# The sums over values ahead of the projections and outputs in TensorE's odd steps

## The reference

```
xn = layernorm(x)
q, k, v = xn @ Wq.T, xn @ Wk.T, xn @ Wv.T          (split into 16 heads)
diff_sq  = max(|q|^2 + |k|^2 - 2 q.k, 0)
cosh_arg = 1 + 2 diff_sq / max((1 - |q|^2)(1 - |k|^2), 1e-6)
attn = softmax(-arccosh(max(cosh_arg, 1)))          (over the 1024 keys)
out  = x + (attn @ v) @ Wo.T + xn @ int4(kernel) + bias + (xn @ a) @ b
```

## Time and profile before

| | |
|---|---|
| median of 3 runs | 2432.23 us (2431.07 to 2434.84) |
| profiled execution | 2431.75 us, of it span 2430.1 us |
| mean granted TensorE clock | 0.993 |
| TensorE (PE) busy | 2259.8 us, 93% |
| ScalarE (ACT) busy | 2166.6 us, 89% |
| VectorE (DVE) busy | 2014.8 us, 83% |
| sum_v matmuls (L223) | 4096, 548.0 us busy |
| sum_one matmuls (L239) | 2048, 270.7 us busy |

### The profile page before, as it was taken

One profiled execution on the slowest core, in us unless ns is written; L12 is line 12 of the kernel. 1 busy time (PEld: TensorE's weight loads), 2 busy tenths in 40 slices (PEclk: granted clock), 3 DMA queues, 4 the chain that ended last, 5 costly groups with the idle time before them and its releaser, 6 DMA issues. The chain is left out here.

```text
span 2430.1 us, 45001 instructions
## 1 busy us (share of the span) xinstructions
PE 2259.8 (93%) x17416; PEld 817.8 (34%) x17416; DVE 2014.8 (83%) x2754; ACT 2166.6 (89%) x2051; POOL 84.5 (3%) x75
## 2 busy tenths in 40 slices
PE   6999999999999999999999999999999999987776
PEld 2433333333333333333333333333333333322222
DVE  7779888888888888888888888888888888876675
ACT  4379999999999998999999999999999999999993
POOL 0100000000000000000000000000000000000000
PEclk9999999999999999999999999999999999999998
DMA  4443334433445443354525344443334454253422
GB/s 154 125 135 84 109 95 130 127 101 108 117 139 130 132 116 91 113 143 126 144 80 137 103 131 135 134 126 105 113 108 144 125 135 109 84 135 91 116 82 80
DMA packets 355425, 285.01 MB, mean 117 GB/s; under 512 B 81132, under 2 KB 294252, under 8 KB 355208
## 3 DMA queue, kind: packets, MB, share of 16 engines
q1 hardware_dynamic: 355208, 282.10, 41.8%
HBM read 159.77 MB, written 121.36 MB: 116 GB/s over the span
## 5 line engine op out<-in xcount | busy, mean ns | idle before, releaser
L508 ACT ACTIVATE root<-pU 128x1024 f32<-128x1024 f32 x1024 | 1030.1, 1027 | 55.3 <-PE pU L211 47.1
L512 ACT ACTIVATE root<-root 128x2048 f32<-128x2048 f32 x512 | 983.1, 1920 | 47.4 <-DVE root L828 46.7
L828 DVE TENSOR_SCALAR root<-root 128x2048 f32<-128x2048 f32 x512 | 625.3, 1221 | 101.5 <-ACT root L508 101.0
L211 PE MATMUL pU<-QS,KS 100*128 100x512 f16 x2048 | 615.7, 383 | 68.9 <-ACT root L508 62.8
L833 DVE TENSOR_TENSOR root<-root 128x2048 f32<-128x2048 f32 x256 | 585.5, 2287 | 43.4 <-PE pO L223 27.1
L223 PE MATMUL pO<-root,VX 128*32 128x512 f32 x4096 | 548.0, 605 | 49.7 <-ACT o_s L518 49.7
L211 PEld LDWEIGHTS pU<-QS,KS 100*128 100x128 f16 x2048 | 145.2, 97 | 602.8 <-ACT root L508 290.6
L239 PE MATMUL pZ<-root,ones 128*32 128x512 f32 x2048 | 270.7, 595 | 0.9 <-DVE root L833 0.9
L291 PE MATMUL pM<-Wqh,xT 128*128 128x512 f16 x480 | 162.8, 383 | 3.1 <-DVE xT L678 1.6
L223 PEld LDWEIGHTS pO<-root,VX 128*32 128x32 f32 x4096 | 84.5, 108 | 233.9 <-issue 223.6
L291 PE MATMUL pM<-Wvh,xT 128*128 128x512 f16 x480 | 161.7, 379 | 0.4 <-DVE Wvl L632 0.4
(11 more groups left out here) (223 smaller groups left out, 2163.2 us busy)
## 6 DMA issues: line engine op xcount, KB each, us to landing
v_d<-v_o SPq DMA_DIRECT2D x64, 264.0 KB, 2.1
k_d<-kx SPq DMA_DIRECT2D x64, 264.0 KB, 2.2
KT<-k_d SPq DMA_DIRECT2D x64, 264.0 KB
VX<-v_d SPq DMA_DIRECT2D x64, 264.0 KB
xts<-in_x SPq DMA_DIRECT2D x32, 512.0 KB, 4.1
res_d<-f_o SPq DMA_DIRECT2D x64, 256.0 KB, 4.0
QS<-qh_d SPq DMA_DIRECT2D x128, 128.0 KB
KS<-kh_d SPq DMA_DIRECT2D x128, 128.0 KB
```

What stands on the lines that cost most here:

```text
L211: mm = pe.matmul(pU[:, col:col + HALF], KS[i][:, h, j * P:(j + 1) * P], QS[i][:, h, half * HALF:(half + 1) * HALF], start=True, stop=True)
L508: act.activation(root[:, q % RING, cols], pU[:, cols], ACT.Square).then_inc(squared, 1)
L512: act.activation(root[:, q % RING, :], root[:, q % RING, :], ACT.Sqrt).then_inc(rooted, 1)
L828: v.tensor_scalar(root[:, q % RING, :], root[:, q % RING, :], CS * CS, CS * CS, ALU.max, ALU.subtract).then_inc(clamped, 1)
```

## The change

In TensorE's program, `behind(p, k)` and the `sum_v` of odd steps change places. Even steps have no `sum_v`, and `sum_one` stays last. No instruction is added, removed or altered, and no other engine's program changes.

```diff
                     distances(0)
                 if s + 1 < 2 * QUADS:
                     distances(s + 1)
-                behind(p, k)
                 if s % 2 and 0 <= (s - 5) // 2 < QUADS:
                     sum_v((s - 5) // 2)
+                behind(p, k)
                 if s % 4 == 1 and 0 <= (s - 7) // 2 < QUADS:
                     sum_one((s - 7) // 2)
```

## The result

The changed kernel takes 2569.67 us (median of 4 runs, 2567.31 to 2570.03), the kernel before 2431.66 us on the same chip: a ratio of 1.0563, 95% interval 1.0544 to 1.0581. 2565 us were forecast, from 2505 to 2592.

The account below looks back on a forecast made before the run. No engine is full; a chain passing between TensorE, ScalarE and VectorE was taken as the bound. 2431.75 us + 98.0 (periods 8 to 55) + 10.5 (periods 1 to 7) + 24.6 (clock) = 2564.9, forecast 2565 us, range 2505 to 2592.

Parts of the forecast that it names:

- The chain enters TensorE at the copies: At ScalarE's pO copies; in period 22 a halved clock made TensorE 1.63 us later, the next copy 1.64 us later.
- Step 5: Six v projection matmuls land behind the wait for the pO copy, delaying step 6's distances: 1.52 us a period.
- Turns: Steps 9 and 13: switching between sums and fp16 matmuls costs two more turns, 0.22 us for each period.
- the late k projection: Step 3, odd periods: k projection ends behind the sums, so ScalarE takes k 0.6 us late, in even-to-odd stretches alone.
- Sum of the stretches: Copy to next copy, 24 even and 24 odd periods: 2.34 and 1.74 us each, 98.0 us together.
- Periods 1 to 7: Periods without outputs: between 0 and 2.34 us each, taken as 1.5, 10.5 us together.
- The clock: Even periods' longer wait drops TensorE's clock in 15 of 23 cases at 1.64 us each: 24.6 us.
- Rival (a): Slower by the other terms, but a 3 us wait does not lower the clock: 2540 us, chance 0.22.
- From period 56 on: Last periods, without projections: nothing stands in step 5, so no loss, 0 us.
- (b): Delay mostly taken back by slack in ScalarE and VectorE: 2468 us, with odd periods' share 2505; chance 0.15.
- (c): Faster: sums end 1.3 us earlier, so VectorE's add_pair waits for them go: 2404.7 us, chance 0.04.
- (d): No difference, because TensorE would idle in step 5 either way: 2432 us, chance 0.04.

Follow-up runs that it names:

- e2: Kernel before with the new order in step 5 alone: 2555.30 us, ratio 1.0511.
- e7: Kernel before with the new order in steps 9 and 13 alone: 2448.66 us, ratio 1.0059.
- e6: Kernel before with the new order in step 3 alone: 2442.28 us, ratio 1.0034.
- e1: Changed kernel with the old order in step 5 alone, the new order in all other odd steps: 2468.41 us, ratio 1.0148 to the kernel before.
- e5: Changed kernel with six extra matmuls, result unread, ahead of step 5's sums in periods 1 to 55: 2548.20 us, ratio 1.0465 to the kernel before.
- e8: Changed kernel with sum_one moved ahead of the product too: 2543.94 us, ratio 1.0449 to the kernel before.
- e9: Changed kernel with the old order from period 56 on: 2560.36 us, ratio 1.0533 to the kernel before.
- e10: Kernel before with the new order from period 56 on alone: 2441.50 us, ratio 1.0041.
- e4: Kernel before with ScalarE's copy of pO one step earlier, in step 4: 2393.91 us, ratio 0.9842.

## Why the prediction was right, point by point

- *The chain enters TensorE at the copies, and a delay behind them is passed on in full.* Right. The accident of period 22 had been the only evidence; the changed kernel repeats it eleven times at 1.6 us each, and e2's three plain stretches are longer by the whole 1.54 us.
- *Step 5: 1.52 us, in even and odd periods.* Right: 3.61 us from the sums to the distances against 3.60. e2's odd-to-even stretches are 34.6 us longer in sum, 1.44 each.
- *Turns, 0.22 us a period, and the late k projection, 0.60.* Right in kind, a little small. e7 measures the turns at 0.33 and 0.24 us, e6 the projection at 0.35 us alone; in e1 the sum is 0.94 instead of 0.82. The 0.26 that e6 and e7 leave fits the turn of step 1, which makes the k projection later still, but no run has that turn alone. ScalarE's wait for k is 0.48 us in the changed kernel.
- *Sum of the stretches.* 2.34 and 1.74 us were forecast; the undisturbed even stretch grew by 2.48 us, the odd ones by 39.7 / 24 = 1.65 in the mean (an undisturbed one by 1.78).
- *Periods 1 to 7.* 13.1 us against 10.5. The price was a guess within 0 and 2.34 us, and its reason, that the copy is waited for in these periods as well, holds in the kernel before for only two of the seven (0.58 us in period 2, 0.20 in period 4).
- *The clock.* Right in kind, too dear in size. Falls in 11 even periods instead of the 15 assumed, each at the price read from period 22. Net of the one fall that the kernel before had, 16.3 us, where 24.6 were in the sum. The mean granted clock of 0.981 misses the sign named in advance, 0.97 or less. Rival (a) held that waits of 3 us do not lower the clock; e5 shows that they do. The wait was 2.72 to 2.99 us, mostly under the 2.9 to 3.1 forecast. The two of three was a guess, and the share of falls isn't set by the length of the wait alone: with 3.08 us and more it was 21 of 23 in e2 and 11 of 23 in e8. e9, with the same code as the changed kernel up to period 55, had 11 falls too, but some in other periods, two of them (10 and 14) behind waits of 2.72 us. What decides beside the length stays open.
- *From period 56 on: 0.* Wrong, and by e9 and e10 worth 9 us. The step of the argument was that nothing stands in step 5 there, and that ScalarE has the chain; it left out that the turns of steps 9 and 13 lengthen TensorE's waits (1.68 instead of 1.49 us), and, as far as argued, that an engine off the chain comes onto it when its clock is halved. This error and the clock's cancelled; without that luck the sum would have been 2574 or 2557.
- *Rivals (b), (c), (d).* Nothing was taken back. ScalarE's wait for the norm fell from 42.8 to 34.4 us only. VectorE's wait for the sums did vanish, from 27.1 to 2.8 us, as (c) had it, and was worth nothing: VectorE waits for squares 174.6 us now, 101.0 before.

## What to carry to other kernels

Work that stands ahead of a wait in an in-order engine's list is free as long as the wait lasts; before moving it, look for which instruction the wait stands at, and count everything that ends up behind it, for the chain takes it at full price. Here the better change was the opposite one, to look at who is being waited for: the copy, one step earlier in ScalarE's list, made the kernel 1.6% faster (e4). And count the turns between kinds of matmul, and whether an idle time gets so long that the clock falls: the turns cost a quarter of a microsecond and come every period, a fall cost 1.6 us and came in 11 of them.

## What the runs showed of the hardware

- Adding 330 useless matmuls, 1.3 us in each of 55 waits, made the kernel 21 us faster (e5 against the changed kernel), since TensorE's granted clock (0.981 to 0.990 in the mean) no longer fell to 1.2 GHz behind the wait.
- In these profiles single waits of the sums up to 1.80 us were not followed by a fall in the projecting periods. Waits of 2.05 and 2.06 us were in some cases (periods 22 of the kernel before and 55 of the changed one) and not in another (period 22 of e6), 2.72 to 2.99 us in 11 of 23, and 3.08 us and more in 21 of 23 (e2) or 11 of 23 (e8). The Trainium skill ("TensorE: Matmul & The Clock Gate", section "Why this matters for your kernels") advises against idle gaps between bursts of matmuls, of a length that among these only e2's and e8's waits reach. The trace agrees in kind, but here shorter waits were followed by falls too.
- A fall costs by how much of the work lies in it: 1.6 us when it begins 0.4 to 1.2 us behind the start of the sums, and in e2, where the sums mostly start at half speed, 1.4 us when the clock is back 3 us behind their start and 2.6 when it takes over 5 us.
- The turn from eight fp32 matmuls in column groups of 32 to fp16 matmuls over all columns and back costs 0.24 to 0.33 us for the pair (e7). The Trainium skill ("TensorEngine Tiling (Array Packing)", section "Key Properties") says that changing the tiling mode drains TensorE; the trace agrees, with 1.00 instead of 0.86 us on the one side and 0.31 instead of 0.22 on the other. The two kinds differ in number format too, and no run separates that from the mode.
